# Packed queries and keys in the dense attention layers, and one product for height and width sums in the position layers

## The reference

```
attn = q * scale @ k
rel_h = einsum('bhwc,hkc->bhwk', q, Rh)      # q at row h, column w
rel_w = einsum('bhwc,wkc->bhwk', q, Rw)
attn = softmax(attn + rel_h[..., :, None] + rel_w[..., None, :])
```

## Time and profile before

| | |
|---|---|
| runs | 1862.83 us median of three, 1848.17 to 1878.35 |
| profiled execution, its span | 1902.0 us (no other time of this execution is given) |
| mean granted TensorE clock | 0.953 of full speed |
| busy share | PE 90%, DVE 39%, ACT 29%, POOL 8% |
| chain that ended last | PE 78%, DVE 13%, ACT 4% |
| instructions, PE / DVE / ACT | 15226 / 1885 / 828 |

### The profile page before, as it was taken

The page is one execution under the profiler, slowest core; times in us unless marked ns, Lnnn a source line. Parts: engine busy times, 40 slices in busy tenths (PEclk is TensorE's granted clock), DMA queues, the critical chain, the costliest instruction groups (busy, mean ns, idle before and its releaser), DMA issues.

```text
span 1902.0 us, 35088 instructions
## 1 busy us (share of the span) xinstructions
PE 1716.1 (90%) x15226; PEld 1338.5 (70%) x15226; DVE 744.8 (39%) x1885; ACT 548.9 (29%) x828; POOL 145.6 (8%) x181
## 2 busy tenths in 40 slices
PE   6989998989998989998898888989899999999898
PEld 5767766767766767766777667888566666667666
DVE  3232234342334333344333333412464563463553
ACT  1132232232232232232232122112334333343332
POOL 1000000000000000000002110102111011010000
PEclk8698999899999999999999988999999999899999
DMA  9500000000000000000000023564100000000000
GB/s 275 233 1 1 1 1 1 2 1 1 1 1 1 2 1 1 1 1 1 1 3 16 22 71 106 159 187 151 30 1 18 9 1 18 9 1 1 9 1 9
DMA packets 28412, 64.37 MB, mean 34 GB/s; under 512 B 4185, under 2 KB 20540, under 8 KB 26499
## 3 DMA queue, kind: packets, MB, share of 16 engines
q1 hardware_dynamic: 19572, 52.01, 8.8%
q0 software_dynamic: 3072, 6.30, 1.1%
q10 hardware_dynamic: 5616, 3.84, 0.6%
HBM read 40.30 MB, written 21.82 MB: 33 GB/s over the span
## 4 chain that ended last, share of the span: by engine, by line
PE 78%; DVE 13%; ACT 4%; issue 2%; DMA 1%; another core or an unknown queue 1%; SPq 0%; POOL 0%; ACTq 0%; DVEq 0%
PE ps L533 65%; DVE neg L1656 6%; PE ps L763 3%; PE ps L753 3%; ACT ring L1157 2%; PE ps L650 2%; PE ps L708 1%; DVE neg L1654 1%; PE ps L605 1%; PE ps L564 1%; PE ps L978 1%; DVE moms L1719 1%; PE ps L593 1%; DMA rw<-rows_by_expert 1%
## 5 line engine op out<-in xcount | busy, mean ns | idle before, releaser
L1157 ACT ACTIVATE ring<-ps 128x1024 f32<-128x1024 f32 (+1 forms) x240 | 232.7, 980 | 430.5 <-PE ps L533 355.5
L1656 DVE TENSOR_REDUCE neg<-ps 128x4 f32<-128x1024 f32 x192 | 234.5, 1225 | 241.2 <-PE ps L533 241.2
L533 PE MATMUL ps<-kz,qt 32*128 32x256 f32 x1152 | 166.3, 415 | 51.3 <-DVE negp L1648 22.6
L533 PE MATMUL ps<-qm,kz 32*128 32x256 f32 x1152 | 167.5, 422 | 4.5 <-ACT pkp L1157 2.4
L533 PEld LDWEIGHTS ps<-kz,qt 32*128 32x128 f32 x1152 | 93.0, 192 | 89.1 <-DVE neg L1656 33.7
L533 PE MATMUL ps<-ident 128*128 128x256 f32 x444 | 142.9, 408 | 11.7 <-DMA lw<-in_lw 11.0
L533 PE MATMUL ps<-xt,lw 97*128 97x256 f32 x480 | 132.6, 428 | 9.7 <-ACT xt L1192 3.6
L1437 POOL TENSOR_TENSOR rstds<-ves,nhalf 128x2 f32<-128x2 f32 x56 | 39.3, 702 | 1200.7 <-DVE ves L1726 1200.7
L533 PE MATMUL ps<-rw,relt 32*128 32x256 f32 (+1 forms) x864 | 122.8, 388 | 0.7 <-ACT xt L1192 0.7
L533 PEld LDWEIGHTS ps<-xt,lw 97*128 97x128 f32 x480 | 96.2, 209 | 36.9 <-issue 9.5
L533 PEld LDWEIGHTS ps<-qm,kz 32*128 32x128 f32 x1152 | 93.0, 195 | 24.3 <-issue 13.0
(11 more groups left out here) (284 smaller groups left out, 2945.7 us busy)
## 6 DMA issues: line engine op xcount, KB each, us to landing
rw<-in_moe SPq DMA_DIRECT2D x39, 384.0 KB, 3.7
rows_by_expert<-late SPq DMA_DIRECT2D x8, 1536.0 KB, 20.6
rw<-rows_by_expert SPq DMA_DIRECT2D x39, 96.0 KB, 3.0
rows_by_expert<-zone ACTq DMA_DIRECT2D x39, 96.0 KB
lw<-in_lw SPq DMA_DIRECT2D x3, 720.0 KB
rw<-in_relw SPq DMA_DIRECT2D x1, 2048.0 KB
lw<-in_moe SPq DMA_DIRECT2D x1, 1920.0 KB
rw<-in_relw SPq DMA_DIRECT2D x1, 1792.0 KB
```

What stands on the lines that cost most here:

```text
L533: return pe.matmul(o, w, m, start=start, stop=stop)
L1157: act.activation(dst, src, ACT.Exp).then_inc(*q.adds("exp_done"))
L1656: ins = dve.tensor_reduce(at, ps[:, b:b + 2, :].rearrange("p j (f k) -> p j f k", f=2), AX.X, ALU.max, negate=True)
```

## The change

**Dense layers (L2, L3, L4).** The weights are laid out anew (`dense_weights`): quad 0 takes the first 16 rows of each 32-row block and quad 1 the second 16, so one product gives both; quad 2 stands alone. Queries are two products of 128 x 256, keys two. All copies of the queries are one VectorE copy of 512 columns (`dense_queries`). Keys are three ScalarE activations of 256 columns (`dense_keys`): the first reads the packed bank with a scale for each partition that is zero in the second half, the second with one that is zero in the first half, so each gives the keys of one quad and zeros elsewhere, and the mark row is put by the bias. `rows_of`, `mark`, `noted` and `values_at` say for each quad where its queries, its mark, its buffer of negated maxima and its values stand. The buffer `neg` is three deep instead of two.

**Position layers (L0, L1).** The query weights are written twice, so that rows 16 to 31 of a block hold the same queries as rows 0 to 15. VectorE then overwrites the second copy with the queries with image rows and columns exchanged (`across`, a predicated copy by a mask of partitions: 512 columns for quads 0 and 1, 256 for quad 2). The table of a position step holds the height table in the first 16 rows and the width table in the second. One product then gives, for image row `at`, the height sums of the positions of row `at` and the width sums of the positions of column `at`. Two of the four steps go, with their two filling products. The width sums stand in other partitions of the same PSUM bank, in the exchanged order; VectorE takes them over the copied height sums by predicated copies that read every sixteenth element (`by_row`), in L1 two of 384 elements, in L0 five, all of them in one piece after both halves are copied. The position tables in memory are half as large. Two small tables are loaded in addition.

The strings that set the order are the same. The core of the diff:

```diff
     def qkv_a(q, l, im):                       # TensorE
+                if l.dense:
+                    quad_b(l, xi, 0, 6, 0)
+                    quad_b(l, xi, 1, 6, NTOK).then_inc(*q.adds("q_mm"))
+                    yield
+                    quad_b(l, xi, 2, 7, 0)
+                    quad_b(l, xi, 3, 7, NTOK).then_inc(*q.adds("k_mm"))
+                    yield
+                    pe.wait_ge(*q.next("q_ready"))
+                    value_rows(l, xi, 6).then_inc(*q.adds("v_mm"))
+                    yield
+                    pe.wait_ge(*q.next("k_ready"))
+                    return
...
-                            last = pe.matmul(o[:, :, k, :], rwt[:, 0, at % l.rel, :], qi[:, :, at, :],
-                                             start=k == 0, stop=True, skip_group_check=True)
-                        last.then_inc(*q.adds("rel_mm"))
-                        yield
-                    for half in range(2):
-                        pe.wait_ge(*q.next("rel_ready"))
-                        fill(ps[:, 6 + half, 0:NTOK])
-                        o = ps[:, 6 + half, 0:QUADS * 128].rearrange("p (s h w) -> p s h w", s=QUADS, h=HH)
-                        for k in range(8):
-                            at = 8 * half + k
-                            last = pe.matmul(o[:, :, :, k], rwt[:, 1, at % l.rel, :], qi[:, :, :, at],
+                            last = pe.matmul(o[:, :, k, :], rwt[:, at % l.rel, :], qi[:, :, at, :],
                                              start=k == 0, stop=True, skip_group_check=True)
...
+            def dense_keys(l, kb, bank):           # ScalarE
+
+                a0 = 0 if l is not L3 else 2
+                act.activation(kb[:, 0, :], bank[:, 0:NTOK], ACT.Identity, scale=keyed[:, a0:a0 + 1], bias=one16[:, 0:1])
+                act.activation(kb[:, 1, :], bank[:, 0:NTOK], ACT.Identity, scale=keyed[:, a0 + 1:a0 + 2],
+                               bias=keyed[:, 4:5])
+                return keys(l, kb[:, 2, :], bank[:, NTOK:T])
...
     def position_sums(q, l, im):               # VectorE
                 def more(dst, z):
-                    return dve.tensor_tensor(dst, z, dst, ALU.add)
+                    return by_row(dst, z, 1 if l.pad else 0)
...
                 for half in range(2):
-                    dve.wait_ge(*q.next("rel_mm"))
-                    z = ps[:, 6 + half, 0:QUADS * 128].rearrange("p (s h w) -> p s h w", s=QUADS, h=HH)
+                    z = ps[:, 6 + half, 0:QUADS * 128].rearrange("p (s w h) -> p s h w", s=QUADS, h=HH)
...
     def qkv_a(q, l, im):                       # VectorE, position layers
+                query = (qn if l.pad else qt[:, im])
+                dve.wait_ge(*q.next("q01_half"))
+                across(query[:, 0:2, :], ps[:, 6, :]).then_inc(*q.adds("q01_ready"))
                 yield
                 dve.wait_ge(*q.next("q2k0_mm"))
-                query_key(l, (qn if l.pad else qt[:, im])[:, 2, :], kz[:, im, 0, :], ps[:, 7, :])\
-                    .then_inc(*q.adds("q2k0_ready"))
+                dve.tensor_copy(query[:, 2, :], ps[:, 7, 0:NTOK]).then_inc(*q.adds("dve_step"))
+                dve.tensor_scalar(kz[:, im, 0, :], ps[:, 7, NTOK:T], l.scale, one16[:, 0:1], ALU.mult, ALU.add)
+                dve.wait_ge(*q.own("dve_step"))
+                across(query[:, 2:3, :], ps[:, 7, 0:NTOK]).then_inc(*q.adds("q2k0_ready"))
...
+            def across(query, bank):
+
+                n = query.shape[1]
+                dst = query.rearrange("p s (h w) -> p s h w", h=HH)
+                turned_q = bank.rearrange("p (s w h) -> p s h w", s=n, h=HH)
+                return by_row(dst, turned_q, 0)
+
+            def by_row(dst, z, which):
+
+                rows = turned_row[:, which:which + 1].unsqueeze(2).unsqueeze(3)
+                return dve.copy_predicated(dst, rows.to_broadcast(list(dst.shape)), z)
+
+            def dense_queries(q, query):
+
+                dve.wait_ge(*q.next("q_mm"))
+                dve.tensor_copy(query[:, 0:2, :].rearrange("p s t -> p (s t)"), ps[:, 6, :]).then_inc(*q.adds("q_ready"))
```

More of the change, by code:

```diff
@@ L72, in __init__ @@
         self.name, self.scale, self.rel, self.pad, self.causal = name, scale, rel, pad, causal
+        self.dense = not rel
+        self.rows_of = (0, 0, 1) if self.dense else (0, 1, 2)
+        self.mark = (HD, 0, HD) if self.dense else (HD, HD, HD)
+        self.noted = (0, 2, 0) if self.dense else (0, 1, 0)
+        self.values_at = 4 * 128 if self.dense else 6 * 128
         kinds = ("pads", "full") if pad else ("full",)
@@ L569, in first_scores @@
                         else:
-                            last = mm(o, qb[r, im, s, hs], kb[r, im, s, :], True, not l.rel)
+                            last = mm(o, qb[r, im, l.rows_of[s], hs], kb[r, im, s, :], True, not l.rel)
                     return last
@@ L649, in shift @@
                     for half in range(2):
-                        last = pe.transpose(ps[:, 5, half * 128:half * 128 + 128], neg[:, s % 2, half, :], ident[:, :])
+                        last = pe.transpose(ps[:, 5, half * 128:half * 128 + 128], neg[:, l.noted[s], half, :], ident[:, :])
                     last.then_inc(*q.adds("neg_mm"))
@@ L1198, in qkv_a @@
             def qkv_a(q, l, im):
+                if l.dense:
+                    yield
+                    act.wait_ge(*q.next("k_mm"))
+                    dense_keys(l, kz[:, im], ps[:, 7, :]).then_inc(*q.adds("k_ready"))
+                    yield
+                    act.wait_ge(*q.next("v_mm"))
+                    keep_values(v[:, im, :, :, 0:HD], ps[:, 6, 0:2 * D]).then_inc(*q.adds("v_ready"))
+                    yield
+                    return
                 act.wait_ge(*q.next("q01_mm"))
@@ L1314, in first_b @@
                     yield
-                act.wait_ge(*q.next("n_k12_mm"))
-                keys(L3, k3[:, im, 1:3, :].rearrange("p s t -> p (s t)"), ps[:, k12_bank, :])\
-                    .then_inc(*q.adds("n_k12_ready"))
-                yield
                 act.wait_ge(*q.next("n_v_mm"))
@@ L1600, in position_sums @@
                         ins.then_inc(*q.adds("rel_ready"))
-                    yield
+                    if not half:
+                        yield
                 if not l.pad:
@@ L1632, in qkv_a @@
                 yield
-                if l.rel:
-                    yield from position_sums(q, l, im)
+                yield from position_sums(q, l, im)
             def paired(q, l, im):
@@ L2013, in first_b @@
                 normalise(q, 1, im, turn_x(q.coming), xn).then_inc(*q.adds("n_rows"))
-                yield
-                yield
-                yield
-                if im:
+                for _ in range(7):
                     yield
-                yield
-                if not im:
-                    yield
-                yield
-                yield
-                yield
             def hidden_b(q, im):
@@ L2239, in program, with dense_weights, put @@
         return {"a": sa.made, "b": sbb.made}
+def dense_weights(w, b):
+    o = np.zeros((CH + 1, 2, WD), np.float32)
+    qk = o[:, :, 0:4 * 128].reshape(CH + 1, 2, 2, 2, QH, 2, HD)
+    def put(dst, z):
+        z = z.reshape(-1, 2, QUADS, QH, HD)
+        for s, (block, half) in enumerate(((0, 0), (0, 1), (1, 0))):
+            dst[:, :, block, :, half, :] = z[:, :, s]
+    for c in range(2):
+        rows = slice(c * CH, (c + 1) * CH)
+        put(qk[0:CH, c], w[rows, 0:2 * D])
+        o[0:CH, c, 4 * 128:] = w[rows, 2 * D:3 * D]
+    if b is not None:
+        put(qk[CH:, 1], b[None, 0:2 * D])
+        o[CH, 1, 4 * 128:] = b[2 * D:3 * D]
+    return o
 def attention_weights(w, b):
@@ L2304, in constants @@
     one16 = (i % 32 == HD).astype(np.float32).reshape(128, 1)
+    first, second = i % 32 < HD, i % 32 >= HD
+    keyed = np.stack([first * L2.scale, second * L2.scale, first * L3.scale, second * L3.scale, i % 32 == 0], 1)
     all_ones = np.ones((128, 128))
```

142 lines of the change are left out of this document (70 added, 72 removed).

## The result

The changed kernel takes 1816.17 us (median of 4 runs, 1810.49 to 1819.77), the kernel before beside it 1860.05 us: a ratio of 0.9738 (95% interval 0.9694 to 0.9783). It is faster by 44 us where 73 were forecast; the time lies in the range (1760 to 1832), above the 1775 to 1805 held likeliest and near the first rival's 1817.

The account below looks back on a forecast made before the run. TensorE, busy 90% of the span, was taken as the bound. Dense 38 plus position 49 less 14 for clock falls gave 73 us, so 1862.83 - 73 = 1790 us; likeliest 1775 to 1805, 8 in 10 from 1760 to 1832.

Parts of the forecast that it names:

- first rival: More clock falls: L1 tails fall too, 12 falls at 3.4 us, 1817 us; chance 0.15 for some 8 more.
- Dense layers, 38 us: L2, L3, L4: two products fewer per layer image, saving 14.4, 9.6 and 14.4 us; ends 22 and 43.
- L3's share: L3's part of the dense sum: step soon held by its exponential, 1.2 us an image, 9.6 us for eight.
- Position layers, 49 us: L0 and L1: two of four steps go, scores start earlier; (3.1 + 2.6 + 3.3 + 3.3) x 4 turns.
- Predicated copies at the addition's price: L0 and L1 tails: a predicated copy of 384 elements costs 557 ns, as the addition of that shape.
- rivals with dear copies: Strided PSUM reads cost double, 1804 to 1831 us, chance 0.07; copies at the reciprocal's price, 1914 us, 0.03.
- the one on the slower side: Predicated copies at the reciprocal's price, 6.3 ns an element: 1914 us; chance 0.03, with smaller mishaps 0.04.
- Exchanges of queries at nothing: Position layers: VectorE's row-column exchange hides under the following product, costing nothing; 10 us if it did not fit.
- I count one fall a turn, 4 x 3.4 = 14 us: At L0's first image, new idle time of 2.1 us brings one clock fall a turn, costing 14 us.
- that of 1.8 us in L1 I count as too short: The new idle time in L1's tails brings no clock fall, so it costs nothing at the clock.
- Scores waiting anyway: Rival: exponentials hold the dense steps, saving 22 us there while the position sum stays; 1806 us, chance 0.1.
- 4.44 - 2.6 = 1.8: L0's second image: of 4.44 us of removed steps only 2.6 counted, because exponentials hold later steps.

Follow-up runs that it names:

- experiment 1: The dense part of the change alone, position layers put back to four steps, additions and old tables: 1843.72 us, ratio 0.9825 to the kernel before.
- experiment 7: The kernel before with only the position part of the change: 1868.05 us, ratio 0.9978.
- filled kernel: The kernel before with fourteen filling products a turn in idle times L0's attention always had: 1865.98 us, ratio 0.9985.
- early scores: Edit moving the wait for the position sums behind the first score products, which do not read them; alone on the changed kernel 1796.99 us.
- experiment 12: The position part alone, with early scores and all filling products in tails, new waits and older L0 idle times: 1802.65 us, ratio 0.9640.
- second profile of before: The kernel before, unchanged, profiled once more: 1868.4 us.
- experiment 2: The changed kernel with filling products ahead of the first scores, four at L0's first image, three at both L1 images: 1809.66 us, ratio 0.9650.
- Experiment 4: The changed kernel with the early scores edit and nothing else: 1796.99 us, ratio 0.9589 to the kernel before.
- experiment 3: Changed kernel with filling products in the L0 and L1 tails, and four more between last steps of L0's first image: 1797.97 us, ratio 0.9596.
- Fourteen fills: Filling products a turn in idle times L0's attention always had: kernel before 1865.98 us, ratio 0.9985; changed kernel 1802.55 us, ratio 0.9667.

## Why the prediction was right, and where its size was off

- **Dense layers, 38 us.** Right: 29 measured and an estimated 10 given back to the clock (experiment 1); 1.73 us an image in L4. L3's share was not measured apart.
- **Position layers, 49 us.** Right on the path: 6 measured and an estimated 46 given back (experiment 7), and 63 against a filled kernel, of which 6 belong to the early scores and 7 to a better clock (99 us low against 116), so 50 are left (experiment 12).
- **Predicated copies at the addition's price.** Right: 554 against 557 ns, strided reads of PSUM included. The rivals with dear copies are out, and with them the one on the slower side. The Trainium skill's sentence on PSUM patterns that are not contiguous ("PSUM — Partial Sum Buffer", Specifications (TRN2)) speaks of matmuls; of VectorE no loss shows here.
- **Exchanges of queries at nothing.** Not tried alone, but in the changed kernel's trace no wait of TensorE ends with an exchange: it waits for VectorE's predicated copies 12 times, 21.6 us together, each time for `relt`, the position sums.
- **The clock: "I count one fall a turn, 4 x 3.4 = 14 us".** This is the term that was mis-sized. It measured some 39 us, 98 us more at the low clock. The fall at L0's tail came in all three steady turns of the changed kernel's profile, for 10.2 us each. (The "eight products" of the prediction's clock rows are eight instructions, four products; before and after are read alike.) Three things were wrong in the count. The first is "that of 1.8 us in L1 I count as too short": waits of 1.64 us there have a fall in three cases of six. The second is the argument against more falls, "the tails lie in stretches in which TensorE is otherwise never idle". In the trace of before TensorE waits 1.56, 0.70, 0.61, 1.74 and 0.72 us within the 17 us behind L0's tail, and a fall of 23.9 us can begin behind the 1.74: it did in the second profile of before, and in experiment 2 with the tail filled. So falls could not be priced at the new tails alone: filling the tails and the new waits gave 25 us, filling idle times that were always there 20, and with both and the early scores the stretch is at 1.00. The third is that the profile of before that I counted from showed that stretch at 0.97, and in a second execution it is 0.91: its being at full speed was no fixed property of the kernel before.
- **What is only argued.** The change takes work out of the L0 stretch (products and fills) and adds waits to it, and no run takes out the work alone. Experiment 4, which shortens the waits and leaves the work as it is, has 39 us less at the low clock than the change, and speaks for the waits. But it is not shown how much the missing work adds.
- **The first rival** (more falls, 1817) is what happened, by number of us and in part by place: it named the L1 tails, and half of them have a fall. But 84 of the 135 us at the low clock begin elsewhere, so that its number comes out is in part luck. "TensorE: Matmul & The Clock Gate" of the Trainium skill (HAM oscillation) tells of a wait for a DMA in each pass, of some 3 to 5 us, after which the next pass starts cold. This case is another one: no wait in the turn shown is longer than 2.13 us, and it has several low stretches all the same.
- **Scores waiting anyway.** In L0's second image yes, by the two new waits of 1.22 and 0.80 us, 2.0 us together; 4.44 - 2.6 = 1.8 of that was in the sum.

What stays open: why the same instructions of the L0 stretch run at 0.97 in one execution and at 0.91 in another, and why the fall behind the same wait comes in one turn and not in the next (experiment 3).

## What to carry to other kernels

Where products are taken out of a stretch with many short waits, the clock of that stretch may fall and take the saving back, as here: check its granted clock, window by window, before and after, in more than one execution, and count the loss beside the path's saving. Work that costs nothing on the path, such as filling products or the first products of the next step, can go into the waits in the same edit; here it made of 3% gained 5%. A part whose measured gain is zero (0.9978) may still be worth some 50 us once that is done.

## What the runs showed of the hardware that was not expected

- An us at the low clock costs an estimated 0.38 to 0.45 us and not a half, by pairs of runs of one kernel; two turns of one execution give 0.41 (experiment 3: 14 us for 34 more at the low clock).
- A stretch of TensorE work with the same instructions has a granted clock of 0.97 in one execution and 0.91 in another, and the runs of the kernel before spread over 26 us as the clock goes down (1849.95 us at 0.977, 1875.71 at 0.959).
- Fourteen fills a turn show no gain in one kernel (0.9985, 0.9933 to 1.0038) and some 20 us in another.
